# Attention body: the fourth unit's scores directly behind the first weighted values, and a projection in front of the second

## The reference, cut to what matters

```
qkv  = modulate(layernorm(x)) @ W_qkv          # q, k, v: 16 heads of 64
attn = softmax(q k^T / 8)                      # per sequence and head, 128 x 128
x    = x + g_msa * ((attn v) @ W_out + b_out)
```

## Time and profile before

| | |
|---|---|
| median of 3 runs | 640.35 us |
| span of the profiled execution | 639.0 us |
| PE busy | 623.2 us, 98% |
| PE weight loads busy | 539.6 us, 84% |
| DVE busy | 509.3 us, 80% |
| ACT busy | 478.6 us, 75% |
| POOL busy | 288.5 us, 45% |

### The profile page before, as it was taken

The page is one execution under the profiler, slowest core; times in us unless marked ns, Lnnn a source line. Parts: engine busy times, 40 slices in busy tenths (PEclk is TensorE's granted clock), DMA queues, the critical chain, the costliest instruction groups (busy, mean ns, idle before and its releaser), DMA issues.

```text
span 639.0 us, 17308 instructions
## 1 busy us (share of the span) xinstructions
PE 623.2 (98%) x5570; PEld 539.6 (84%) x5570; DVE 509.3 (80%) x1118; ACT 478.6 (75%) x1721; POOL 288.5 (45%) x353
## 2 busy tenths in 40 slices
PE   8999999999999999999999999889998999999996
PEld 8788888888888898888888888779987888888885
DVE  6889877887878788878787886978866888888876
ACT  4997887877877978778778788768786656565652
POOL 2445253444343443534434524446554345544551
PEclk9999999999999999999999999999999999999999
DMA  7301012011010110110111102023342121222101
GB/s 234 88 21 46 10 48 52 9 45 42 19 45 16 45 45 8 45 47 14 45 28 33 45 1 62 18 60 107 115 125 66 50 69 46 54 66 66 40 26 34
DMA packets 54675, 32.50 MB, mean 51 GB/s; under 512 B 15201, under 2 KB 52465, under 8 KB 54641
## 3 DMA queue, kind: packets, MB, share of 16 engines
q1 hardware_dynamic: 53008, 27.85, 16.0%
q0 software_dynamic: 1632, 4.21, 2.0%
HBM read 25.74 MB, written 6.31 MB: 50 GB/s over the span
## 4 chain that ended last, share of the span: by engine, by line
PE 91%; DVE 6%; ACT 1%; issue 1%; DMA 0%; DVEq 0%; ACTq 0%
PE banks L618 10%; PE banks L644 9%; PE banks L629 8%; PE banks L1924 7%; PE banks L589 7%; PE banks L593 5%; PE banks L590 5%; PE banks L1337 4%; PE banks L602 3%; PE banks L1896 3%; PE banks L1910 3%; PE banks L604 2%; PE banks L603 2%; PE banks L1884 2%; PE banks L664 2%; PE banks L665 2%
## 5 line engine op out<-in xcount | busy, mean ns | idle before, releaser
L536 POOL TENSOR_TENSOR late_blocks<-late_blocks,p_rsum 128x512 f32<-128x512 f32 x128 | 130.5, 1040 | 219.2 <-DVE p_rsum L960 219.2
L832 ACT ACTIVATE late_blocks<-banks,neg_max 128x128 f32<-128x128 f32 x512 | 182.4, 391 | 0.8 <-DVE neg_max L953 0.8
L832 ACT ACTIVATION_READ_ACCUMULATOR late_blocks<-banks,neg_max 128x1 f32 x512 | 119.2, 233 | 0.0
L810 ACT ACTIVATE wide<-banks 128x512 f32<-128x512 f32 x126 | 77.6, 616 | 39.8 <-PE banks L593 34.7
L973 DVE CAST oT_hi<-banks 128x512 fp32r<-128x512 f32 x60 | 41.5, 691 | 62.3 <-PE banks L644 62.3
L589 PE MATMUL banks<-xT_hi,w_qkv_hi 128*128 128x256 f32 x256 | 82.8, 324 | 0.0
L953 DVE TENSOR_REDUCE neg_max<-banks 128x8 f32<-128x1024 f32 x64 | 77.1, 1205 | 2.2 <-PE banks L618 1.0
L618 PE MATMUL banks<-wide 64*128 64x128 f32 x1024 | 74.4, 285 | 0.0
L593 PE MATMUL banks<-xT_hi,w_qkv_lo 128*128 128x256 f32 x256 | 72.1, 282 | 0.0
L590 PE MATMUL banks<-xT_lo,w_qkv_hi 128*128 128x256 f32 x256 | 71.9, 281 | 0.0
L618 PEld LDWEIGHTS banks<-wide 64*128 64x128 f32 x1024 | 62.1, 187 | 10.7 <-issue 7.9
(11 more groups left out here) (171 smaller groups left out, 1554.9 us busy)
## 6 DMA issues: line engine op xcount, KB each, us to landing
early<-in_mask SPq DMA_DIRECT2D x16, 220.0 KB
early<-in_mask SPq DMA_DIRECT2D x80, 44.0 KB
x_in<-in_x SPq DMA_DIRECT2D x16, 128.0 KB, 2.2
x_res<-in_x SPq DMA_DIRECT2D x16, 128.0 KB, 2.2
x_scratch<-x SPq DMA_DIRECT2D x16, 128.0 KB, 1.9
f_x_in<-x_scratch SPq DMA_DIRECT2D x16, 128.0 KB, 2.4
f_x_res<-x_scratch POOLq DMA_DIRECT2D x16, 128.0 KB, 2.9
x_scratch<-f_x POOLq DMA_DIRECT2D x16, 128.0 KB, 2.2
```

The source lines that it names most:

```text
L536: pool.tensor_tensor(p[:, par, heads, :], p[:, par, heads, :], p_rsum[:, par, heads].unsqueeze(2).broadcast_to([128, 4, T]), ALU.mult).the ...
L810: act.activation(dst, proj_ps[k % 2], ACT.Copy).then_inc(proj_saved[k % 2], 1)
L832: act.activation(p[:, par, m, :], s_ps[par][:, e, j, :], ACT.Exp, bias=neg_max[:, par, 4 * e + j:4 * e + j + 1], accum_out=p_sum[:, par, m ...
```

## The change

In TensorE's `body`, `scores(i, 3, ...)` moves ahead of `turn_back(i)`, directly behind `probs_v(i, 0)`; and `project_qk(i, QK1[0])`, task 8, moves ahead of `probs_v(i, 1)`, so that the scores of unit 4 follow that step directly. Nothing else is changed: no instruction is added or taken away, and the other engines' queues stay as they are.

```diff
             probs_v(i, 0)
+            scores(i, 3, i - 1, QK1)
+
             if more(i, -1):
                 turn_back(i)
-
-            scores(i, 3, i - 1, QK1)
             if nxt:
                 pe.wait_ge(xT_split, i * 2 + 4)
                 project_qk(i, QK0[0])
...
             if nxt:
                 for k in QK0[1:]:
                     project_qk(i, k)
+                project_qk(i, QK1[0])
             probs_v(i, 1)
 
             if nxt:
-                project_qk(i, QK1[0])
                 scores(i, 4, i, QK0)
```

## The result

The changed kernel takes 649.78 us (median of four runs, 649.49 to 650.0), the kernel before 640.42 us beside it: ratio 1.0143, 95% interval 1.0129 to 1.0158. It is slower by 9.4 us; the forecast was 649.5. The profiled execution has a span of 648.3 us against 639.0.

A forecast was written before the change was run, and what follows sets the result against it. TensorE, 98% busy, was taken as the bound. A loss of 0.60 us in each of bodies 1 to 14 (8.40) plus 0.78 in body 0 gave +9.18 us, so 649.5 us; range 645.3 to 652.8.

The forecast's parts named there:

- The turn back behind S3: TensorE: two transposes moved behind unit 3's scores take 0.21 us, not 0.37; the following work comes 0.18 us earlier.
- VectorE's residual addition: VectorE's addition that reads the moved transposes: no delay, or 0.05 us; its readers would not see 0.1 us.
- The two changes of form: TensorE: joining projection 8 to projection 7 removes two switches between matmul forms, saving 0.19 us.
- the bank wait: Projection 8 waits for ScalarE to copy projection 6 out of the same PSUM half: TensorE stands 0.38 us.
- T2 behind the split: Unit 2's transposes wait for VectorE's split of unit 1's weighted values, 2.60 us from their start: a 0.49 us stand.
- The margin at W2: Unit 2's weighted values get VectorE's copy of the transposed probabilities just in time, by 0.03 to 0.18 us.
- Rival D: At unit 2's weighted values the margin is not held, VectorE being late: +0.3 on top, 654 us; chance 0.06.
- A: Both waits are hidden and TensorE keeps 0.37 us a body: 635.0 us, faster; chance 0.05.
- B: Only the bank wait occurs, unit 2's transposes find their area free: +0.11 us a body, 642.2 us; chance 0.05.
- C: The stand at unit 2's transposes is real but partly given back: about +0.40 us a body, 646.4 us; chance 0.05.
- E: Many short stands lower TensorE's clock from projection 8 to unit 2's transposes: 45 us more, 695 us; chance 0.01.

The follow-up runs named there:

- the run with the groups exchanged: Changed kernel, with unit 2's second group of probability transposes issued ahead of its first: 647.59 us, ratio 1.0120 to the kernel before.
- both side edits: Changed kernel, with ScalarE's copy of task 6 ahead of unit 3's first exps and unit 2's transpose groups swapped: 640.95 us, ratio 1.0005.
- the chain shortened: Changed kernel with four edits: both side edits, VectorE's later-pair statistics ahead of the split, task 7's copy two exps earlier: 637.19 us, ratio 0.9947.

## Why the prediction was right

The time was 0.3 us off, and the loss per body 0.62 us against 0.60. Both waits that the prediction added up are in the trace, on the lines it named, and the runs that take them away one by one show that they make the loss. That the sum came out so close has some luck in it, since single steps were up to 0.1 us off and partly cancelled. Step by step:

- **The turn back behind S3.** Predicted 0.18 us less, measured 0.19 in the run of this part alone. The median of that run has 1.9 us less by its ratio where 2.5 was the sum, inside the interval.
- **VectorE's residual addition**, said to be delayed by 0 to 0.05. This was wrong: in the changed kernel it starts 0.80 us behind the second split part (105.44, 106.24), and where nothing is waited for the next instruction comes 0.61 behind it (113.07, 113.68), so the transposes hold it for 0.19. VectorE follows them 0.35 us behind the next group's start (105.89, 106.24), not by the 0.1 that I had read from W1. The rows before had a nearer case: behind transposes ScalarE starts 0.28 us after the next group (112.33, 112.61). It costs nothing, for the reason given: the row maximum ends at 107.9 and ScalarE's exps stand behind the copy of 108.46.
- **The two changes of form, and the bank wait.** Predicted a stand of 0.38, measured 0.38. W1 lies 7.62 us behind W0 (103.58, 111.20), where the prediction's 109.48 less 101.83 is 7.65. The prediction's opening calls all margins under half a microsecond; this one was not, with 0.79 us from the copy's end to projection 8, as its own working says.
- **T2 behind the split.** Predicted 2.60 us from W1, measured 2.71. The step that was short is the signal, taken from ScalarE as 0.05; from the end of VectorE's second part (113.07 + 0.69) to T2's first matmul it is 0.15. What that added was mostly given back: T2 to W2 is 2.37 us (113.91, 116.28) where 2.43 was assumed, and W1 came 0.03 earlier. 0.11 less 0.06 less 0.03 is the 0.02 by which the loss per body was off.
- **The margin at W2.** The chain through VectorE, put within 0.03 to 0.18 us of deciding, does decide as soon as T2's wait is gone: 4.98 us against 5.08, 0.10. The total was right by cancelling: in the run with the groups exchanged VectorE's copy starts 4.06 us behind W1 (110.24, 114.30) where 4.27 was reckoned (109.48, 113.75), and from its end to W2 there are 0.24 us where the signal was put at 0.05. Rival D, that it lengthens the change's own loss, did not come.
- **The rivals.** A, the full gain, came only with four further edits to what PE waits for, and then not whole: 0.5%, not 0.8%. That T2's wait was harmless (B) is excluded: the trace has it in 15 bodies, it stays when the bank wait goes, and both side edits were needed to come back to the kernel before. C, that part is given back before the body's end, did not come: the body is 0.62 us longer, and the wait at the last value projection is 6.6 us over 16 times in both kernels. The clock did not fall (E): it is granted at 1.00 in the body with both stands.

## What to carry to other kernels

When a full engine's queue is reordered to save its own time, write down for each result the distance from its producer to its next user, on both sides of the move, and hold it against the latency of the engine that works in between. Here the starts of projections 7 and 8 came together from 1.93 to 0.81 us, 1.12 less, against a margin of 0.74: a wait of 0.38. W1 and T2 came together from 3.01 to 2.11, 0.90 less, against a margin of 0.30 (3.01 less the 2.71 that the split takes): a wait of 0.60. The second part saved 0.19 us a body and cost 0.98. And look for a second chain of nearly the same length before removing the first: here taking away T2's wait of 0.60 us gave back 0.10 a body, 1.5 us in all, since a chain of 4.98 us lay beside the one of 5.08.

## What the runs showed of the hardware

- Six matmuls of 256 columns between two groups of another form take 0.90 us. Two such sixes apart take 1.81 us (0.91 and 0.90), joined 1.61 (107.27 to 108.88 with the chain shortened). Two transposes take 0.37 us between weighted values and scores but 0.20 between scores and a projection.
- The way out of a projection's PSUM half is 0.96 us from the last matmul's start, of which 0.60 is the copy. In this order the other half's projection covers 0.82 of it, and 0.14 is left as a wait.
- PE's granted clock stayed at 1.00 in a body with 0.73 us of 25.92 without matmuls, in stands of up to 0.6 us.
- The time from a copy's end to the TensorE group that waits for it was not one number: 0.05 us to a projection (106.59, 106.64), 0.15 to the transposes of T2 (113.76, 113.91), and 0.24 to weighted values (114.98, 115.22).
